# A post-norm decoder block: bias seeds by ScalarE, sums and shifts at other places, norm scales on GpSimd

## The reference

```
q, k = rope(x Wq), rope(x Wk)                       # 16 heads of 16 numbers
attn = q k^T * SCALE + min(pos_k - pos_q, 0) * slope[h] * 8
out  = softmax(attn) v;   x = layernorm(x + out Wp + b)
x = layernorm(x + cross_attention(x, ctx))
x = layernorm(x + top-2 of 8 experts(x))            # gelu, weights from a softmax
layernorm(x) = (x - mean) / sqrt(var + 1e-5)        # over the 256 numbers of a row
```

## Time and profile before

| | us |
|---|---|
| median of 3 runs | 1904.31 |
| profiled execution | 1906.57 |
| its span | 1904.8 |
| PE busy (matmuls) | 1745.0 |
| DVE (VectorE) busy | 1390.0 |
| ACT (ScalarE) busy | 1174.9 |
| POOL (GpSimd) busy | 355.5 |
| self attention, heads | 157 to 863 |
| projection, norm, start of cross attention | 863 to 950 |
| cross attention, heads | 950 to 1521 |
| projection, norm, routing | 1521 to 1590 |
| experts and last norm | 1590 to 1905 |

### The profile page before, as it was taken

One profiled execution on the slowest core, in us unless ns is written; L12 is line 12 of the kernel. 1 busy time (PEld: TensorE's weight loads), 2 busy tenths in 40 slices (PEclk: granted clock), 3 DMA queues, 4 the chain that ended last, 5 costly groups with the idle time before them and its releaser, 6 DMA issues.

```text
span 1904.8 us, 30266 instructions
## 1 busy us (share of the span) xinstructions
PE 1745.0 (92%) x10422; PEld 906.8 (48%) x10422; DVE 1390.0 (73%) x2786; ACT 1174.9 (62%) x2401; POOL 355.5 (19%) x577
## 2 busy tenths in 40 slices
PE   6989999999999999988799999999999877999993
PEld 3433333333333333325444444444444266999993
DVE  7587999999999999914699999999999053010113
ACT  1214777777777777785148777777787842333333
POOL 8120222242222222111000000000000003333331
PEclk9986999999999999999879999999999977999997
DMA  7232000000100000011203001001012126777773
GB/s 261 104 130 73 28 28 28 28 27 32 35 31 31 31 31 28 2 42 63 92 1 101 33 24 39 29 27 40 24 34 78 45 94 188 193 209 194 205 186 105
DMA packets 72880, 141.78 MB, mean 74 GB/s; under 512 B 14156, under 2 KB 47325, under 8 KB 70509
## 3 DMA queue, kind: packets, MB, share of 16 engines
q1 hardware_dynamic: 65018, 129.48, 20.6%
q0 software_dynamic: 7712, 10.37, 3.4%
HBM read 110.71 MB, written 28.45 MB: 73 GB/s over the span
## 4 chain that ended last, share of the span: by engine, by line
PE 73%; DVE 11%; ACT 7%; issue 4%; DMA 3%; SPq 1%; POOL 0%; POOLq 0%; ACTq 0%; DVEq 0%
PE banks L995 21%; PE banks L982 21%; PE banks L940 8%; PE banks L1187 7%; PE banks L1197 7%; ACT XT L1257 5%; PE banks L886 4%; DVE skip L1444 2%; ACT late L1257 2%; DVE wset L1444 2%; DVE CM L1440 2%; DMA oper<-qD 2%; PE banks L951 1%; PE banks L894 1%; DVE banks L1472 1%
## 5 line engine op out<-in xcount | busy, mean ns | idle before, releaser
L1257 ACT ACTIVATE XT<-banks 128x512 f32<-128x512 f32 x1240 | 658.3, 603 | 229.5 <-PE banks L982 160.4
L940 PE MATMUL banks<-oper 52*128 52x512 f32 (+1 forms) x2048 | 712.4, 441 | 32.0 <-DVE CM L1444 12.6
L982 PE MATMUL banks<-oper 54*128 54x512 f32 x1856 | 673.3, 451 | 28.6 <-POOL oper L755 10.5
L982 PEld LDWEIGHTS banks<-oper 54*128 54x128 f32 x1856 | 302.6, 186 | 514.0 <-ACT XT L1257 305.5
L1435 DVE TENSOR_REDUCE CM<-banks 128x1 f32<-128x402 f32 x1024 | 512.8, 566 | 21.1 <-PE banks L940 9.3
L940 PEld LDWEIGHTS banks<-oper 52*128 52x128 f32 x2048 | 347.8, 191 | 139.5 <-DVE CM L1444 63.6
L1257 ACT ACTIVATE late<-banks 128x512 f32<-128x512 f32 x616 | 328.3, 604 | 85.7 <-PE banks L982 71.3
L995 PE MATMUL banks<-XT,VS 128*32 128x512 f32 x2480 | 334.4, 611 | 6.8 <-ACT XT L1257 6.1
L1615 DVE TENSOR_TENSOR YB<-banks,b2E 128x256 f32<-128x256 f32 x39 | 16.5, 424 | 250.0 <-PE banks L1197 250.0
L1336 ACT ACTIVATE HID<-banks,b1E 128x128 f32<-128x128 f32 x312 | 85.1, 381 | 181.3 <-DMA b1E<-in_b1T_dram 169.4
L995 PE MATMUL banks<-late,VS 128*32 128x512 f32 x1232 | 164.9, 607 | 2.9 <-ACT late L1257 2.6
(11 more groups left out here) (205 smaller groups left out, 1393.8 us busy)
## 6 DMA issues: line engine op xcount, KB each, us to landing
W<-in_w1T_dram SPq DMA_DIRECT2D x39, 1024.0 KB
oper<-kD SPq DMA_DIRECT2D x32, 256.0 KB
W2R<-in_w2T_dram SPq DMA_DIRECT2D x8, 1024.0 KB, 7.9
oper<-kxD SPq DMA_DIRECT2D x32, 208.0 KB
b2E<-in_b_dram SPq DMA_DIRECT2D x39, 128.0 KB
qD<-parts SPq DMA_DIRECT2D x8, 512.0 KB, 2.7
kD<-parts SPq DMA_DIRECT2D x8, 512.0 KB, 2.7
oper<-kD SPq DMA_DIRECT2D x32, 128.0 KB
```

The lines of the kernel that those rows point to most:

```text
L940: mm = pe.matmul(slot[:, n * QB:n * QB + ch], QO[64 * g:64 * g + M_ROWS, c2, col:col + P], KO[64 * g:64 * g + M_ROWS, c2, k0:k0 + ch], sta ...
L982: pe.matmul(bank, KO[64 * g:64 * g + S_ROWS, c, b * P:(b + 1) * P], QO[64 * g:64 * g + S_ROWS, c, q0:q0 + QB], start=True, stop=True).then ...
L1257: act.activation(PT[(c * plan.nu + u) % PRING], score_bank(plan, u, h, c), ACT.Exp).then_inc(A.exps, 1)
```

## The change

1. ScalarE writes `DB` into the diagonal's 128 columns of S0's bank before S0, after the third exponential of the block before (`seeded`). S0 becomes two or three matmuls: the diagonal's columns, which add onto what is there, and those left and right of them. VectorE's addition goes. Exempt are block 0 of head 0 and all of head 15, which keep VectorE's addition.
2. The `sum` item stands first in block 2, with a sequence of its own for this block; in other blocks of self attention the fifth m is gone from the sequence, so that a fifth beat (`shift`) comes behind S3.
3. The three steps that join a head's maxima are written at the start of block 11 (of block 10's end for head 14).
4. ScalarE saves the last head's output after the third exponential of block 0 and the seed, ahead of the fourth.
5. Norm scales: GpSimd adds epsilon, negates the mean, raises to the power -0.5 and multiplies, four steps per group; the root on ScalarE and the seven steps on VectorE go, and the aggregates don't wait for each other.

```diff
 def sequence(self, b):
+        if self.causal and b == SUM_AT:
+            return "S0 m S1 m m S2 m V0 S3 m".split()
...
-            items.append(("sum", 0, 0, -1, None))
+            items.insert(0 if self.causal else len(items), ("sum", 0, 0, -1, None))
...
-SELF = Plan(TT, QB, True, False, 1, {2: "m S0 m S1 m S2 m V0 m S3"})
+SELF = Plan(TT, QB, True, False, 1, {2: "m S0 m S1 m S2 m V0 S3"})
...
+        def seeded(h, b):
+            return h < H - 1 and (h, b) != (0, 0)
...   GpSimd, both calls of group norms; the last norm has the same four steps
+            def group_scales(call):
+                for g in range(NG):
+                    p, n = g % 2, call * NG + g
+                    pool.wait_ge(s_grp, GT4 * (n + 1))
+                    if n >= 2:
+                        pool.wait_ge(s_xn, GT4 * (n - 1))
+                    pool.tensor_scalar(varG[:, p, 0, :], aggG[:, p, :, 1], EPS, None, ALU.add).then_inc(s_gsd, 1)
+                    pool.tensor_scalar(varG[:, p, 1, :], aggG[:, p, :, 0], -1.0, None, ALU.mult).then_inc(s_gsd, 1)
+                    pool.wait_ge(s_gsd, 3 * n + 2)
+                    pool.tensor_tensor(varG[:, p, 4, :], varG[:, p, 0, :], inverse_root[:, :].to_broadcast([P, GT4]), ALU.pow).then_inc(s_gsd, 1)
+                    pool.wait_ge(s_gsd, 3 * (n + 1))
+                    pool.tensor_tensor(varG[:, p, 5, :], varG[:, p, 1, :], varG[:, p, 4, :], ALU.mult).then_inc(s_gsc, 1)
+                    pool.wait_ge(s_gsc, n + 1)
...   PE
+                    if alibi and u % 4 == 0 and seeded(h, u // 4):
+                        pe.wait_ge(A.seeded, TT * h + u // 4)
...
-                    pe.matmul(bank, KO[...], QO[...], start=True, stop=True).then_inc(A.scores, 1)
+                    cuts = [(0, QB)]
+                    if alibi and n == 0 and seeded(h, b):
+                        d = b % 4 * P
+                        cuts = [cut for cut in ((d, d + P), (0, d), (d + P, QB)) if cut[0] < cut[1]]
+                    for i, (lo, hi) in enumerate(cuts):
+                        mm = pe.matmul(bank[:, lo:hi], KO[64 * g:64 * g + S_ROWS, c, b * P:(b + 1) * P],
+                                       QO[64 * g:64 * g + S_ROWS, c, q0 + lo:q0 + hi],
+                                       start=(i > 0 or len(cuts) == 1), stop=True, skip_group_check=True)
+                    mm.then_inc(A.scores, 1)
...   ScalarE
-                        if A is SA and u % 4 == 0:
-                            act.wait_ge(A.biased, TT * h + (u // 4 + 1))
+                        if A is SA and u % 4 == 0 and not seeded(h, u // 4):
+                            act.wait_ge(A.biased, 1 if h == 0 else 2 + u // 4)
...
-                        if u == 3 and not first:
+                        if A is SA and u % 4 == 2:
+                            h2, b2 = h + (u + 2) // plan.nu, (u + 2) // 4 % plan.nb
+                            if seeded(h2, b2):
+                                c2 = h2 % RING
+                                if b2 == 0:
+                                    act.wait_ge(A.v, h2 + 1)
+                                act.wait_ge(A.exps, plan.nu * h + u)
+                                act.activation(score_bank(plan, 4 * b2, h2, c2)[:, b2 % 4 * P:(b2 % 4 + 1) * P], DB[:, c2, :],
+                                               ACT.Copy).then_inc(A.seeded, 1)
+                        if u == (2 if A is SA else 3) and not first:
                             save(h - 1)
...   VectorE
-                        if alibi:
+                        if alibi and not seeded(h, b):
                             tile = score_bank(plan, 4 * b, h, c)[:, b % 4 * P:(b % 4 + 1) * P]
...
+                        if b == plan.nb - LEAD and h + 2 < H:
+                            head_maxima(h + 1, pos + off - 1)
...   and in the group norms
                     for q in range(GT4):
-                        link(dve.bn_aggr(aggG[:, p, q, :], statsG[:, q, :]), s_ln)
-                    dve.tensor_scalar(varG[:, p, 0, :], aggG[:, p, :, 1], EPS, None, ALU.add).then_inc(s_grp, 1)
-                    dve.wait_ge(s_gsd, call * NG + g + 1)
-                    (the reciprocal and five more steps)
+                        ins = dve.bn_aggr(aggG[:, p, q, :], statsG[:, q, :])
+                        ins.then_inc(s_grp, 1)
```

More of the change, by code:

```diff
@@ L460, in __init__ @@
                 self.biased = sem(f"{name}_diagonal_biased")
+                self.seeded = sem(f"{name}_diagonal_seeded")
                 self.chain = sem(f"{name}_shift_chain")
@@ L705, in _ @@
             pool.memset(zeros[:, :], 0.0)
+            pool.memset(inverse_root[:, :], -0.5)
             pool.wait_ge(s_zero, 2)
@@ L804, in _ @@
             pool.wait_ge(SA.pv, SELF.nb * H)
+            group_scales(0)
             attention(XA, CROSS, VX)
@@ L867, in _ @@
                                             YS[:, i % 2, j, :], None, compute_op=ALU.add).then_inc(s_add, 16)
+            for g in range(TT // 4):
+                c = slice(4 * g, 4 * g + 4)
+                pool.wait_ge(s_varF, 4 * (g + 1))
+                pool.tensor_scalar(varF[:, 0, c], aggF[:, c, 1], EPS, None, ALU.add).then_inc(s_sdF, 1)
+                pool.tensor_scalar(varF[:, 1, c], aggF[:, c, 0], -1.0, None, ALU.mult).then_inc(s_sdF, 1)
+                pool.wait_ge(s_sdF, 3 * g + 2)
+                pool.tensor_tensor(varF[:, 4, c], varF[:, 0, c], inverse_root[:, :].to_broadcast([P, 4]), ALU.pow).then_inc(s_sdF, 1)
+                pool.wait_ge(s_sdF, 3 * (g + 1))
+                pool.tensor_tensor(varF[:, 5, c], varF[:, 1, c], varF[:, 4, c], ALU.mult).then_inc(s_nF, 1)
+                pool.wait_ge(s_nF, g + 1)
         @block.tensor
@@ L964, in scores_bank @@
                 def scores_bank(u, h, c):
-                    if h == H - 1 and WIDE <= u < WIDE + 2 * RSLOTS:
+                    if alibi and u % 4 == 0 and seeded(h, u // 4):
+                        pe.wait_ge(A.seeded, TT * h + u // 4)
+                    elif h == H - 1 and WIDE <= u < WIDE + 2 * RSLOTS:
                         pe.wait_ge(A.freed, plan.ring_before(H))
@@ L981, in scores_unit @@
                     g, q0 = qb // 2, qb % 2 * QB
-                    pe.matmul(bank, KO[64 * g:64 * g + S_ROWS, c, b * P:(b + 1) * P], QO[64 * g:64 * g + S_ROWS, c, q0:q0 + QB],
-                              start=True, stop=True).then_inc(A.scores, 1)
+                    cuts = [(0, QB)]
[7 more added lines that the diff above has]
+                    mm.then_inc(A.scores, 1)
                 def pv_batch(b, h, c, part=0):
@@ L1287, in transposes @@
                     p = g % 2
-                    act.wait_ge(s_grp, call * NG + g + 1)
-                    act.activation(varG[:, p, 1, :], varG[:, p, 0, :], ACT.Sqrt).then_inc(s_gsd, 1)
                     if g + 2 < NG:
@@ L1341, in _ @@
             for g in range(TT // 4):
-                cols = slice(4 * g, 4 * g + 4)
-                act.wait_ge(s_varF, g + 1)
-                act.activation(varF[:, 1, cols], varF[:, 0, cols], ACT.Sqrt).then_inc(s_sdF, 1)
-                if g:
-                    normalize(g - 1)
-            normalize(TT // 4 - 1)
+                normalize(g)
         @block.vector
@@ L1421, in attention, with head_maxima @@
                 ch = plan.chunk
+                def head_maxima(h, pos):
+                    n = 2 * h
+                    dve.wait_ge(A.freed, pos + 1)
+                    dve.tensor_reduce(NM[:, :], CM[:, :, 0:2 * (3 - plan.beats)], AX.X, ALU.max, negate=True).then_inc(A.chain, 1)
+                    dve.wait_ge(A.chain, n + 1)
+                    dve.tensor_copy(SHW[:, 0:TT].bitcast(F32R), NM[:, :]).then_inc(A.chain, 1)
+                    dve.wait_ge(A.chain, n + 2)
+                    dve.tensor_tensor(SHW[:, TT:2 * TT].bitcast(F32R), NM[:, :], SHW[:, 0:TT], ALU.subtract).then_inc(A.cols, 1)
                 def ring_item(item, pos, bank, h, c):
@@ L1445, in ring_item @@
                                                      ALU.add, ALU.max, CM[:, a, b:b + 1]).then_inc(A.freed, 1)
-                        if edge == "last":
-                            n = (h + ahead) * 2
-                            dve.wait_ge(A.freed, pos + 1)
-                            dve.tensor_reduce(NM[:, :], CM[:, :, 0:2 * (3 - plan.beats)], AX.X, ALU.max, negate=True).then_inc(A.chain, 1)
-                            dve.wait_ge(A.chain, n + 1)
-                            dve.tensor_copy(SHW[:, 0:TT].bitcast(F32R), NM[:, :]).then_inc(A.chain, 1)
-                            dve.wait_ge(A.chain, n + 2)
-                            dve.tensor_tensor(SHW[:, TT:2 * TT].bitcast(F32R), NM[:, :], SHW[:, 0:TT], ALU.subtract).then_inc(A.cols, 1)
                     elif kind == "shift":
@@ L1475, in step @@
                             off += 1
+                        if b == plan.nb - LEAD - 1 and h + 2 == H:
+                            head_maxima(h + 1, pos + off - 1)
                 pos = 0
@@ L1481, in attention @@
```

(3 more changed lines are left out.)

26 lines of the change are left out of this document (4 added, 22 removed).

## The result

The changed kernel takes 1916.41 us (median of 7 runs, 1909.04 to 1919.95), the kernel before 1904.70 beside it (7 runs, 1903.47 to 1910.68): ratio 1.0048, 95% interval 1.0031 to 1.0066. It is slower, by 9.1 us by the ratio (the medians are 11.7 apart), where 1908.2 us and +3.9 were predicted. The profiled execution of it is 1916.41 with a span of 1914.7, against 1906.57 and 1904.8 before, so the two traces differ by 9.9 us. The 1916.41 lies outside the 1903 to 1914 that the prediction gave to its own mechanism, and inside its whole range of 1887 to 1924.

A forecast was written before the change was run, and what follows sets the result against it. In self attention, 2.60 us per block was put to a TensorE-ScalarE loop the bias doesn't touch. Self attention +14, seeds +0.7, norm scales -4.4, last norm -6.4 sum to +3.9: 1908.2 us, range 1887 to 1924 (some 0.8).

The forecast's parts named there:

- its own mechanism: Whole kernel: the prediction's main account, without its rivals, giving 1903 to 1914 us; chance 0.45.
- Sum first, and the new tokens: Self attention, blocks 2 and 3: the sum's slot and a beat behind S3 delay the maxima, +1.5 us per head.
- Rival B: Blocks 2 and 3: the sum costs nothing in its new place, self attention 21 us better, 1887; chance 0.22.
- Seeds: Self attention: nothing in plain blocks, about 0.15 us each won in blocks 5 and 13, 0.7 taken for ScalarE's copies.
- S0 in cuts: Seeded S0: extra matmuls lie in slack in plain blocks, cost 0.12 us each in blocks 4 and 12.
- Shift behind S3: Block 11 loses its 0.4 us; block 12 gets +0.1 besides the cuts, +0.23 with them.
- Save ahead of the fourth exponential: Saving the head's output earlier, in the next head's block 0: 0 to -0.1 us per head, 0.1 taken.
- Head 15: Last head of self attention: gains some 0.5 us, as its S0 of block 3 no longer waits for the sum.
- Norm scales: First and second norm: shorter VectorE groups (under 4.6 us), TensorE next bound, 2.2 us won in each call.
- Last norm: End of kernel: groups of 2.3 us, last activations ending at 1896.2 instead of 1902.62, -6.4 us (bounds -4.5 and -6.8).

The follow-up runs named there:

- a1: Changed kernel with block 2's old order put back (sum's transposes last, ahead of S3); ratio 0.9960 to the kernel before.
- b5: Changed kernel with the second beat of block 4's first maximum moved ahead of S0, in self attention alone; ratio 1.0049 to the kernel before.
- a3: Changed kernel without seeds and cuts and with block 2's old order; ratio 0.9971 to the kernel before.
- a4: Changed kernel with each seeded S0 issued as one matmul that overwrites the bias, copies and waits kept; ratio 1.0061 to the kernel before.
- b3: Kernel before, with GpSimd waiting at its very end for the last normalized row and clearing a tile of zeros; ratio 1.0022 to the kernel before.
- b6: Changed kernel with self attention's sum last in block 3 and the last four tiles' norm scales back on VectorE and ScalarE; 1889.12 us, 0.9919 of before.
- b7: Changed kernel with the power in the last norm replaced by a multiplication of the same operands; ratio 1.0068 to the kernel before.
- b1: Changed kernel with self attention's sum moved from first in block 2 to last in block 3; 1891.46 us, 0.9927 of before.
- b2: Changed kernel with two beats of block 2 moved, the last one ahead of PV and S3, the sum still first; ratio 0.9999 to the kernel before.
- a2: Changed kernel without seeds and cuts, VectorE adding the diagonal bias again, new block order kept; median 1925.04 us, ratio 1.0097 to the kernel before.

## Why the prediction was right, and where it wasn't

The sign was right, and so was the place of the loss in self attention (blocks 2 and 3). The size was too small: +3.9 against +9.1 by the ratio and +9.9 between the two traces. The miss is made of sizes that went both ways, some of them by the clock that the profiled executions happened to get. By the prediction's own steps:

- *Sum first, and the new tokens*: right, in each of its times; in its cause for block 3, and only in part for block 2. Transposes 0.8 (0.72), slot read 2.2 (2.12), S3 3.65 (3.60), the wait's end 5.6 (5.65), S3 of block 3 7.3 (7.30). +1.5 a head; a1 gives 1.49. In block 3 TensorE stands for 0.94 for the slot, as the step says. In block 2 the step has the second maximum's beat wait for the sum's slot until 2.25. It starts at 2.18, but S2 stands at 2.11, so that wait is 0.07 of the 0.41 that the block lost against the old order. Rival B is refuted by the beat and by S3 of block 3 at 7.30; by what it named as deciding, the slot of the sum, it was nearly even: read at 2.12, wanted at 2.11.
- *Seeds*: "worth nothing in a plain block" was right, and the copy is 0.31 (0.28 predicted). The 0.7 us that the sum had for the copies didn't show: plain blocks stayed at 2.61. The 0.15 in block 5 was wrong: the step took the bias's wait for the cause of VectorE's lateness. b5 shows the cause, the second beat of the first maximum behind S0, which waits for GpSimd; the bias only sat in a gap that was there anyway. In block 13 the 0.15 came (2.86 to 2.72), and the seeds' own share of it is 0.04 (a3 against a1).
- *S0 in cuts*: 0.12 in each of blocks 4 and 12 was too much for those (0.02 and 0.04 by a4) and left out block 2 (0.06) and 5 (0.03): 0.24 predicted, 0.18 measured (for 24 added matmuls a head, 359 in all and not 358). The Trainium skill says in "TensorE: Matmul & The Clock Gate", The mechanism, that a weight load overlaps a running matmul only when the row groups differ. The first two cuts, at 447.21 and 447.35 above, are 0.14 apart, less than one load of these operands takes in the trace (0.18), so this trace does not agree with it, as the earlier trace rows did not.
- *Shift behind S3*: block 11 lost 0.40 as predicted; block 12 went to 3.20 where 3.01 + 0.23 were predicted. Without the seeds it would have been 3.52.
- *Save ahead of the fourth exponential*: block 1 wins 0.15, block 0 loses 0.10. The predicted -0.1 a head is -0.05.
- In all the mean beat is 1.19 longer where 1.05 was predicted (1.17 in a plain head; three beats were 0.1 to 0.3 longer than the others): 2.0 us over 14 heads. Block 5 is 0.17 a head of it, and block 4, 0.10 better than predicted, takes some back.
- *Head 15* was to gain 0.5 and gained nothing: 39.19 from its first exponential to its save, against 39.15. With the 0.7 that the copies didn't cost this makes self attention some 1.8 worse than forecast (+16.6 instead of +14.7).
- *Norm scales*: the mechanism and the size were right, and one of the two didn't show. Groups 4.57 apart, TensorE next. Where the clock is alike in both (b3 and a1, full clock in the first stretch) the first norm takes 32.43 and 30.08 from head 15's save to the last row of the norm: -2.35, predicted -2.2. In the profiled pair it was -0.7, since the clock was at the lower level for longer in the changed kernel. The second norm gave 33.09 - 30.17 = 2.9 in the profiled pair and 32.43 - 30.17 = 2.3 between b3 and a1; that the stretch around it came out 1.0 better than predicted goes with the clock again (0.77 against 0.74); by b3 it gained 1.1 to 2.1.
- *Last norm*: the failed step of the sum. The power was taken as 0.2 and is 1.04, inside its bounds, for 0.7 us to the last row (12.77 against 12.1). And the step counted to the last activation alone, as if the rest behind it stayed as in the kernel before. GpSimd's queue needs 6.72 us to drain behind its last instruction; while its last work ended at 1878.0 that was free, at 1907.5 it ends the kernel. That is 2.9 of the 3.5 us that are missing, and it puts the step as a whole (-2.8) outside its bounds of -4.5 and -6.8.

So 6 us were mis-sized: 2.9 for the drain, 0.7 for the power, 1.8 for the clock in the first norm, 1.9 in self attention, less 1 for the stretch of the second norm. Of these the drain is a mechanism that the prediction left out. The two that hang on the clock are luck of the profiled executions.

## What to carry to other kernels

An item of a ring can cost more than its own length, since in program order its slot makes later items wait (0.94 in block 3 here): work the tokens of the block through to the slot's release, and see what no longer lies beside what, before moving one. Taking work from an engine that isn't the bound gave nothing in the plain blocks here, and a gap in which that work happened to sit isn't proof that the work made it: look at what the gap waited for. Before moving a step to another engine at the end of a kernel, read how long that engine's queue takes to close. Before reading a difference of a few us from two single traces, compare their granted clocks stage by stage.

## What was not expected of the hardware

- GpSimd's closing drain: 6.72 us (changed kernel, b6, b7), 6.95 (b3), 8.51 (before). Counted from the end of GpSimd's last instruction it is nearly one length: it ends 6.93 us behind it in the changed kernel, 6.94 in b6, 6.73 in b3, and 6.73 in the kernel before, where the last indirect transfer is issued within the 8.51. The drains of ScalarE (2.10 in the changed kernel, 2.99 before) and VectorE (0.41 and 0.20) run alongside their last instructions and end 0.03 to 0.05 behind them.
- GpSimd's power of 128x4 elements: 1.04 us, about five times an addition or multiplication of that size (0.20 to 0.24).
- The first 9 us behind self attention come in three lengths from head 15's save to VectorE's first statistics, whatever the order: 9.32 (a1, a3, a4, b1, b2, b3, b5, b6), 11.70 (before, a2, b7) and 13.38 (changed), with a granted clock of 1.00, 0.66 and 0.54 in the windows shown. Which execution gets which, the runs don't tell; it moves a comparison of single traces by up to 4 us, more than a norm's whole gain.
- The same holds for longer stretches. From head 15's save to the first save of cross attention the traces take 136.3 us at a mean granted clock of 0.87 (a3), 141.1 at 0.83 (a1), 142.4 at 0.82 (changed) and 145.4 at 0.80 (a2), all with the same code there. The saves of cross attention took 519.1 and 519.0 in b5 and b7, at 0.98, and 512.4 to 512.6 at 1.00 in all the others.
